# A neighbourhood-attention block whose TensorE program for attention becomes a loop

## What is computed

```python
x = x + attention(layernorm(x))         # 12 heads of 16; each query sees its 7 x 7 neighbourhood and 16 registers
t = x.reshape(-1, 192)
n = layernorm(t)
gate = softmax(n @ gate_w.T)            # 16 experts, the best two per token
y = sum over those two of gate * w2[e] @ (silu(w1[e] @ n) * (w3[e] @ n))
z = sw2 @ (silu(sw1 @ n) * (sw3 @ n))   # shared expert, 1024 wide
out = t + y + z
```

## Time and profile before

| | |
|---|---|
| median of three runs | 1367.69 us (1355.18 to 1371.36) |
| profiled execution | 1353.01 us, its span 1351.2 us |
| TensorE busy, share of the span | 1183.0 us, 88% |
| VectorE, ScalarE, POOL busy | 481.2, 364.4, 571.4 us |
| mean granted TensorE clock | 0.887 |
| transfers | 160.81 MB, mean 119 GB/s |

### The profile page before, as it was taken

The page is one execution under the profiler, slowest core; times in us unless marked ns, Lnnn a source line. Parts: engine busy times, 40 slices in busy tenths (PEclk is TensorE's granted clock), DMA queues, the critical chain, the costliest instruction groups (busy, mean ns, idle before and its releaser), DMA issues. The chain is left out here.

```text
span 1351.2 us, 41755 instructions
## 1 busy us (share of the span) xinstructions
PE 1183.0 (88%) x17206; PEld 962.0 (71%) x17206; DVE 481.2 (36%) x1066; ACT 364.4 (27%) x1271; POOL 571.4 (42%) x688
## 2 busy tenths in 40 slices
PE   5874886986888788788899999999999999999991
PEld 3432675775776676675576767769999999999991
DVE  3432543553554555456622222222222222222220
ACT  2322533443443434341111111111222222222220
POOL 4633543353544535310066660002555555554542
PEclk9987776676877878678999999999999999999996
DMA  5866325225262343310001121235888888888864
GB/s 129 175 163 152 70 69 95 57 68 90 67 106 59 86 87 98 90 41 16 9 17 36 36 83 43 64 122 141 223 221 229 220 221 228 215 220 217 218 162 120
DMA packets 126392, 160.81 MB, mean 119 GB/s; under 512 B 31936, under 2 KB 97248, under 8 KB 126016
## 3 DMA queue, kind: packets, MB, share of 16 engines
q1 hardware_dynamic: 104576, 137.18, 36.9%
q0 software_dynamic: 20336, 20.81, 9.9%
q10 hardware_dynamic: 1296, 0.17, 0.1%
HBM read 129.89 MB, written 31.83 MB: 120 GB/s over the span
## 5 line engine op out<-in xcount | busy, mean ns | idle before, releaser
L679 POOL DMA_INDIRECT acc_dram<-ys,lists x87 | 137.7, 1583 | 283.1 <-DVE ys L1068 180.2
L1357 PE MATMUL ps<-xa,w13r 128*128 128x128 f32 x1392 | 169.7, 275 | 0.3 <-ACT xa L790 0.3
L744 ACT ACTIVATE probs<-ps,nmax 128x156 f32<-128x156 f32 x432 | 162.7, 403 | 8.7 <-DVE nmax L885 8.4
L1357 PEld LDWEIGHTS ps<-xa,w13r 128*128 128x128 f32 x1392 | 162.3, 192 | 0.5 <-issue 0.5
L1061 DVE TENSOR_TENSOR m_h<-m_sg,ps 128x512 f32<-128x512 f32 x87 | 59.8, 688 | 288.8 <-ACT m_sg L796 288.8
L1279 PE MATMUL ps<-xT_all,sw13a_sb 64*128 64x384 f32 x768 | 145.9, 491 | 4.8 <-DVE s_h L1034 4.5
L1162 PE MATMUL ps<-kd,qr 28*32 28x156 f32 x3456 | 102.2, 360 | 46.2 <-issue 40.4
L564 POOL TENSOR_TENSOR kd<-kr,maskp 128x420 f32<-128x420 f32 x144 | 140.3, 1008 | 0.0
L1373 PE MATMUL ps<-w_sb,m_h 128*128 x696 | 136.4, 339 | 0.0
L885 DVE TENSOR_REDUCE nmax<-ps 128x6 f32<-128x936 f32 x72 | 81.5, 1132 | 120.1 <-PE ps L1162 118.9
L1373 PEld LDWEIGHTS ps<-w_sb,m_h 128*128 128x128 f32 x696 | 110.7, 189 | 10.7 <-issue 0.3
(11 more groups left out here) (151 smaller groups left out, 1553.7 us busy)
## 6 DMA issues: line engine op xcount, KB each, us to landing
w13r<-in_w13a SPq DMA_DIRECT2D x87, 512.0 KB
w13r<-in_w13b SPq DMA_DIRECT2D x87, 256.0 KB
vm<-v_dram SPq DMA_DIRECT2D x144, 94.5 KB
w_sb<-in_w SPq DMA_DIRECT2D x8, 768.0 KB, 4.8
vr<-v_dram SPq DMA_DIRECT2D x144, 42.0 KB
kr<-k_dram SPq DMA_DIRECT2D x24, 198.0 KB, 6.5
xn_dram<-xn SPq DMA_DIRECT2D x36, 128.0 KB, 2.8
a_x<-in_x SPq DMA_DIRECT2D x12, 288.0 KB, 3.5
```

Of the source, the lines that this page charges most:

```text
L679: nc.gpsimd.indirect_dma_start(acc_dram, bass.IndirectOffsetOnAxis(ap=lists[:, j, 0:1], axis=0), ys[:, j % V8, :], None, compute_op=ALU.ad ...
L744: ins = nc.scalar.activation(probs[:, n % 2, h, :], ps[:, 2 * half + b, NKEY * g:NKEY * (g + 1)], ACT.Exp, bias=nmax[:, half, b, g:g + 1], ...
L1357: mm(ps[:, g + k, 128 * f:128 * (f + 1)], w13r[:, j % RING, k, 128 * f:128 * (f + 1)], xa[:, j % 2, 0:128], start=f == 0, stop=False, skip ...
```

## The change

TensorE's turns 4 to 33 become a loop (`pe.Fori`) over pairs of turns, with four turns ahead of it and five behind written out. Buffer numbers must repeat after two tiles for that, so `kd`, `vm`, `vr` and `xn2` become two deep. Waits in the loop compare with registers that count tiles. Queries no longer come by the band with pattern rows in place. ScalarE writes them tile by tile into `a_q`, SP, ScalarE and POOL store them to a `q_dram` that has all 128 rows of each tile, the pattern rows are written there once, and one transfer a tile brings 128 full rows to `qt`. The gate's product is formed with the gate as the weight that is held and tokens as what streams, so that no address of a held weight depends on a register; it lands as 16 x 128 in `gT`, and 36 transposes at the end give `logits`. In SP's list x of band n+3 stands ahead of the stores of band n, values are loaded at band 6 for two tiles, and the shared expert's weights have a place of their own and are loaded before attention instead of at turn 30. The diff, cut to its core:

```diff
-        kr = [place("kr0", [128, 3, KBAND], f32, at)]
-        qr = [place("qr0", [128, 3, NC * 128], f32, at)]
-        early = at[0]
-        kr.append(place("kr1", [128, 3, KBAND], f32, at))
-        qr.append(place("qr1", [128, 3, NC * 128], f32, at))
-        kd = place("kd", [128, 3, 4, 3, NKEY], f32, at)
-        vm = place("vm", [128, 3, 4, D], f32, at)
-        vr = place("vr", [128, 3, 4, D], f32, at)
+        sw13a_sb = place("sw13a_sb", [128, 2, SINTER], f32, at)
+        sw13b_sb = place("sw13b_sb", [128, SINTER], f32, at)
+        sw2_sb = place("sw2_sb", [128, 8, D], f32, at)
+        after_sw = at[0]
+        kr = [place(f"kr{u}", [128, 3, KBAND], f32, at) for u in range(2)]
+        qt = place("qt", [128, 2, 3, 128], f32, at)
+        kd = place("kd", [128, 2, 4, 3, NKEY], f32, at)
+        vm = place("vm", [128, 2, 4, D], f32, at)
+        vr = place("vr", [128, 2, 4, D], f32, at)
...
+        def store_q(eng, j, a, g):
+
+            at0 = 64 * (a % 2) + HD * g
+            eng.dma_start(q_dram[NC * j:NC * (j + 1), 32 * g:32 * g + HD, a, :].rearrange("c d y -> d c y"),
+                          a_q[at0:at0 + HD, j % 2, a // 2, :, :]).then_inc((a_sqp if a == 2 else a_sq)[j % 2], 16)
+
+        def queries_stored(eng, j):
+            eng.wait_ge(a_sq[j % 2], A_SQ * (j // 2 + 1))
+            eng.wait_ge(a_sqp[j % 2], A_SQP * (j // 2 + 1))
...
-                u, j, half = n % 2, n // 2, 64 * (n % 2)
-                sp.wait_ge(a_ce[0], n + 1)
-                sp.dma_start(q_dram[0:128, j, :, half:half + 64],
-                             a_f[:, u, 0, :].rearrange("p (c y) -> p c y", c=NC)).then_inc(a_sto[u], 16)
+                u, at0 = n % 2, PADT + BAND * n
                 sp.wait_ge(a_ce[1], 2 * n + 2)
-                sp.dma_start(q_dram[128:192, j, :, half:half + 64],
-                             a_f[0:64, u, 1, :].rearrange("p (c y) -> p c y", c=NC)).then_inc(a_sto[u], 16)
-                at0 = PADT + BAND * n
-                sp.dma_start(k_dram[0:64, at0:at0 + BAND], a_f[64:128, u, 1, :]).then_inc(a_sto[u], 16)
+                sp.dma_start(k_dram[0:64, at0:at0 + BAND], a_k[64:128, u, 0, :]).then_inc(a_sto[u], 16)
                 sp.wait_ge(a_ce[2], n + 1)
-                sp.dma_start(k_dram[64:192, at0:at0 + BAND], a_f[:, u, 2, :]).then_inc(a_sto[u], 16)
+                sp.dma_start(k_dram[64:192, at0:at0 + BAND], a_k[:, u, 1, :]).then_inc(a_sto[u], 16)
                 sp.wait_ge(a_vev, 3 * n + 3)
                 sp.dma_start(v_dram[PADT + n * BAND:PADT + (n + 1) * BAND, :].rearrange("(s p) d -> p s d", p=128),
                              a_v[:, u, :, :]).then_inc(a_sto[u], 16)
@@ -386,31 +397,32 @@
                 if j == 0:
                     sp.wait_ge(s_pad, N_PAD)
                     sp.wait_ge(s_kz, 2)
-                    sp.wait_ge(s_qpat, 2)
                 if j >= 2:
                     sp.wait_ge(b_kd, NC * (j - 1))
-                    sp.wait_ge(b_S[0], NC * (j - 1))
-                    sp.wait_ge(b_S[1], NC * (j - 1))
                 for g in range(4):
                     sp.dma_start(kr[j % 2][32 * g:32 * g + HD, :, :],
                                  k_dram.rearrange("(a g d) t -> g d a t", a=3, d=HD)[
                                      g, :, :, QT * SIDE * j:QT * SIDE * j + KBAND]).then_inc(b_kld[j % 2], 16)
-                for g in range(4):
-                    sp.dma_start(qr[j % 2][32 * g:32 * g + HD, :, :],
-                                 q_dram.rearrange("(a g d) j c y -> g d a j (c y)", a=3, d=HD)[
-                                     g, :, :, j, :]).then_inc(b_qld[j % 2], 16)
+
+            def load_q(m):
+                if m % NC == 0:
+                    queries_stored(sp, m // NC)
+                if m >= 2:
+                    sp.wait_ge(b_S[0], m - 1)
+                    sp.wait_ge(b_S[1], m - 1)
+                sp.dma_start(qt[:, m % 2, :, :], q_dram[m]).then_inc(b_qld[m % 2], 16)
...
             for n in range(NB):
-                store(n)
                 if n + 3 < NB:
                     load_x(n + 3)
+                store(n)
+                if n % 2:
+                    for g in range(4):
+                        store_q(sp, n // 2, 0, g)
+                if n == 1:
+                    sp.wait_ge(s_qpat, 1)
+                    for g in range(4):
+                        sp.dma_start(q_dram[:, 32 * g + HD:32 * g + 32, :, :].rearrange("m p a y -> p m (a y)"),
+                                     pat_q[32 * g + HD:32 * g + 32, :].unsqueeze(1).broadcast_to([16, NT, 3 * 128])
+                                     ).then_inc(s_pq, 16)
...
                 if n == 4:
                     load_band(0)
                 if n == 5:
+                    sp.wait_ge(s_pq, 64)
+                    for m in range(2):
+                        load_q(m)
+                if n == 6:
+                    for m in range(2):
+                        load_v(m)
+                if n == 8:
                     for m in range(3):
                         load_patch(m)
-                if n == 7:
-                    for m in range(3):
-                        load_v(m)
             load_band(1)
...
+                if 2 <= n + 1 < NT:
+                    load_v(n + 1)
...
-                if m >= 3:
-                    pool.wait_ge(b_S[0], m - 2)
-                    pool.wait_ge(b_S[1], m - 2)
+                if m >= 2:
+                    pool.wait_ge(b_S[0], m - 1)
+                    pool.wait_ge(b_S[1], m - 1)
...
+                if n % 2:
+                    pool.wait_ge(a_ce[1], 2 * n + 2)
+                    for g in range(4):
+                        store_q(pool, n // 2, 2, g)
...
+                if u:
+                    act.wait_ge(a_ce[0], n + 1)
+                    for g in range(4):
+                        store_q(act, j, 1, g)
...
-                    v.tensor_copy(logits[:, n - 4, :], ps[:, 7, 448:448 + E]).then_inc(b_lg, 1)
+                    v.tensor_copy(gT[:, 128 * (n - 4):128 * (n - 3)], ps[0:E, 7, 0:128]).then_inc(b_lg, 1)
...
+            dve.wait_ge(b_lgT, 1)
+            v.tensor_copy(logits[:, 0:32, :], ps[:, 0, :].rearrange("p (n e) -> p n e", e=E))
+            v.tensor_copy(logits[:, 32:NT, :], ps[:, 1, 0:E * (NT - 32)].rearrange("p (n e) -> p n e", e=E)
+                          ).then_inc(b_logits, 1)
...
+            def scores(m, p, i, half):
+                if half == 0:
+                    pe.wait_ge(b_kd, m + 1)
+                    pe.wait_ge(b_qld[p], 16 * i + 16)
+                if type(m) is not int or m:
+                    pe.wait_ge(b_e[half], m)
+                pe.sem_inc(passed_pe, 1)
                 for g in range(3):
                     for a in range(4):
...
+            def gate(m):
+                pe.wait_ge(b_xTev, m + 1)
+                cols = ds(m * 128, 128)
+                mm(ps[0:E, 7, 0:128], gate_sb[:, 0, :], xT_all[:, 0, cols], start=True, stop=False)
+                mm(ps[0:E, 7, 0:128], gate_sb[:, 1, :], xT_all[:, 1, cols], start=False, stop=True).then_inc(b_G, 1)
...
+            def turn(n, k, i):
+
+                def is_tile(m):
+                    return type(m) is not int or 0 <= m < NT
+
+                t, u, w, nxt = n - 1, n - 2, n - 3, n + 1
+                i_t, i_nxt = (i - 1, i) if k == 0 else (i, i + 1)
+                if is_tile(t):
+                    probs_T(t, 1 - k, 0)
+                    probs_T(t, 1 - k, 1)
+                if is_tile(u):
+                    roots(u, k)
+                if is_tile(t):
+                    probs_T(t, 1 - k, 2)
+                    probs_T(t, 1 - k, 3)
+                if is_tile(nxt):
+                    scores(nxt, 1 - k, i_nxt, 0)
+                if is_tile(u):
                     project(u)
-                if 0 <= t < NT:
-                    values(t)
-                if 0 <= w < NT:
-                    token_T(w, u)
-                if n + 1 < NT:
-                    scores(n + 1, 1)
-                if 0 <= w < NT:
+                if is_tile(t):
+                    values(t, 1 - k, i_t)
+                if is_tile(w):
+                    token_T(w, 1 - k, u if is_tile(u) else None)
+                if is_tile(nxt):
+                    scores(nxt, 1 - k, i_nxt, 1)
+                if is_tile(w):
                     gate(w)
+
+            scores(0, 0, 0, 0)
+            scores(0, 0, 0, 1)
+            for n in range(4):
+                turn(n, n % 2, n // 2)
+            with pe.Fori(2, NT // 2 - 1) as i:
+                for k in range(2):
+                    turn(2 * i + k, k, i)
+            for n in range(NT - 2, NT + 3):
+                turn(n, n % 2, n // 2)
+
+            pe.wait_ge(b_lg, NT)
+            for m in range(NT):
+                ins = tr(ps[:, m // 32, E * (m % 32):E * (m % 32 + 1)], gT[:, 128 * m:128 * (m + 1)],
+                         ident_sb[0:E, 0:E])
+            ins.then_inc(b_lgT, 1)
```

221 lines of the change are left out of this document (100 added, 121 removed).

## The result

The changed kernel takes **1266.61 us** in the median (four runs, 1263.43 to 1270.45), the kernel before 1369.53 us (four runs, 1355.18 to 1386.82). The ratio is 0.928, with a 95% interval of 0.920 to 0.936. The forecast was 1245 us, between 1204 and 1325. The profiled execution has a span of 1266.5 us, against 1351.2. Some executions of a kernel are slower than its others by one per cent or more (the ninth experiment's profiled one is among them), and the ratios in this document leave those out, so that they differ a little from the quotient of the medians.

What follows compares the result with a forecast made beforehand. Bound: attention's 28 turns, where TensorE waits for 16 KB instruction blocks and its clock falls behind the stops. 1353.0 - 117 + 3 (loop entry) - 8 + 6 + 5 = 1242, forecast as 1245 us median, range 1204 to 1325.

Steps and rivals of the forecast that it cites:

- The loop: Attention's 28 turns: TensorE keeps the pass, a turn falls from 13.77 to 9.60 us, saving 117 us (66 to 138).
- nine more register and wait instructions: In each looped turn: extra instructions of the loop, taken at 0.76 us on top of 8.84 us.
- every pass misses: Rival, loop: each of 14 jumps back pays a block fetch, stops and clock stay; 1407 us, chance 0.13.
- The stops go and the clock stays: Rival, attention's turns: fetch stops vanish but the clock stays low, 12.0 us a turn; 1309 us, chance 0.19.
- Loads of x ahead of the stores: Projection: x asked for one store earlier, gain of 8 us, between 25 gained and 15 lost.
- the stop ahead of the eleventh band: Sign in projection: this TensorE stop should be gone if the forecast is right.
- the pattern transfers: Projection, band 1: four transfers, 3.54 MB, at least 13 us of all transfer engines, with x of band 5 queued behind.
- A stop near the fifth band: Sign in projection: a stop there may be new.
- pattern rows cost more: Rival, projection: x of band 5 late by 15 us, start of attention by 12; 1271 us, chance 0.06.
- Start of attention: Ahead of the first scores: POOL's last query stores, then keys, delay attention; +6 us, between 0 and 12.
- gate: End of attention: 36 transposes and two copies, uncovered; +5 us, at most 5.9 + 1.4 us.
- the weights ahead of tile 2's queries: Start of attention: 2 MB of shared weights stand ahead of these queries; 8 us, half of it hidden.

Runs made afterwards that it cites:

- the ninth experiment: Changed kernel with pattern rows written band by band from DRAM, shared weights in eleven pieces, token numbers earlier, normalising and POOL's last query stores later: 1240.20 us, ratio 0.902.
- the fifth experiment: Changed kernel with VectorE's two normalising instructions of a turn moved behind oT and the third copy of probabilities: 1252.81 us.
- Experiments 3 and 10: Changed kernel with a loop body of four turns: 1430.81 us; changed kernel with the scores' second half formed four times in looped turns: 1596.32 us.
- experiment 11: Changed kernel with one added wait ahead of project in each looped turn, for normalised tokens to land in DRAM, no fetch added: 1375.75 us.
- experiments 2 and 7: Changed kernel with pattern rows kept in SBUF and queries in four transfers: 1239.36 us; the same with x loaded behind the stores again: 1257.42 us.
- the fourth experiment: Changed kernel with VectorE's four steps on token numbers moved from behind the last band to band 8: 1267.55 us.

## Why the prediction was right, and where it was not

**The loop: right in mechanism, low in size.** TensorE keeps the pass, "issue" stops vanish, the queue moves 69 blocks, and the clock is 1.00. The 28 turns gave 129.8 us for a forecast of 117: 52.2 are stops (70.0 idle us became 17.8), 77.6 the clock, since the same matmuls went from 318.0 to 240.3 us. I had 9.60 us a turn, where 9.22 were measured: 8.84 and 0.76 for nine more register and wait instructions. Those cost nothing that shows, as the fifth experiment's 8.67 us with all of them tells. What does cost is 0.63 us of waiting for VectorE, the engine that I named as having the least room, but for a reason that I didn't see: its normalising is held by POOL's additions, so TensorE's turn hung on POOL's.

The Trainium skill, "SBUF — State Buffer", section "Who interferes with whom", says that `tensor_scalar` can enter a mode in which VectorE takes the port pair that it shares with GpSimd, and that whichever of the two starts second is blocked for the other's whole instruction. The rows agree in kind: 980 and 721 ns in the loop, 7.67 us at attention's start. The Trainium skill speaks of one instruction of the other engine; the 7.67 us spanned eight additions, and no run here shows why none of the gaps between them let VectorE in.

**The jump back: the rival's rule was real, its condition was not met.** I gave *every pass misses* 0.13 because no row told what is kept. Experiments 3 and 10 show it at 12 and at 9 blocks; at 7 it doesn't occur. The Trainium skill, "Runtime: NRT & Kernel Launch", section "Instruction fetch mechanics", gives TensorE's instruction memory 2048 instructions in one sentence, and in another, on taken branches of any engine, a window of two pages. The 1306 instructions that stayed speak against two pages; the 1882 that were fetched anew on nine blocks show that the number of instructions alone doesn't decide. From the 128 KiB of the Trainium skill an estimate is eight blocks of the 16 KB in the earlier trace rows; the runs set what is kept between 7 and 9.

**The clock: right, and shown.** "The stops go and the clock stays" is refuted by the clock of 1.00, and experiment 11 shows the other side: stops of 55 us in all that fetch nothing cost another 50 us in slower matmuls.

**Loads of x ahead of the stores: the step that failed.** I took a gain of 8 us, from +25 to -15, and got a loss of 20.6 us in projection. The order of SP's list is worth 11 to 13 us by experiments 2 and 7, and the stop ahead of the eleventh band is gone, as I said; the value loads, now at band 6, leave one of 4.1 us ahead of the tenth. The mis-sized term is the pattern transfers: I priced 3.54 MB at the last stage's 206 GB/s, "at least 13 us", and used that lower bound as the upper end too. The transfers moved with everything else 113 GB/s at a share of 0.90, and the stop was 38.2 us. The row that I took has large pieces into 128 partitions; these were pieces of 1536 bytes out of 16. A stop near the fifth band was among the signs that I listed, and the rival *pattern rows cost more* had the place; its 1271 us lie nearer the result than my 1245, but with 23 us lost in projection where 28.6 us were missing, and without the turns' extra gain.

**Start of attention and gate: near in size, one for the wrong reason.** +7.5 us for +6 at the start, but the query stores ahead of POOL's keys were not what TensorE waited for; it was VectorE's held instruction. My other term there, the weights ahead of tile 2's queries, cost nothing in the changed kernel, where TensorE came no earlier than the queries; the fourth experiment shows it at 6.05 us of stop. (2 MB at 206 GB/s are 9.7 us, not the 8 that I wrote.) The end cost 11.5 us for 5. Between the last `project` and the shared expert are 13.5 us against 6.6, and the 36 transposes are most of that, with the copies behind them:

```profile
534.26 4.02 PE L1324 MATMUL ps<-ident_sb,gT 16*128 16x16 f32 x36 [0.37 <-DVE gT L937]
539.19 1.65 PE L1338 MATMUL ps<-xT_all,sw13a_sb 64*128 64x384 f32 x4 [0.91 <-DVE logits L1082]
```

That is 6.9 us for the gate, within its bounds. The other 4.6 us of the end are in the written-out turns behind the loop, which are fetched and stop as before; why they took 29.8 us where they had taken 25.2, no run shows.

By the table the span lies 26.3 us above the forecast's sum: 28.6 in projection, 1.5 at the start, 2.3 in the first turns, 6.5 at the end and 0.2 behind it, less 12.8 gained in the turns. So the forecast was near in part by luck: a gain in the turns that I had too small made up for nearly half of the loss in projection that I had not seen.

## What to carry to other kernels

Where TensorE stops in the middle of runs of small matmuls with nothing late, count the blocks that its program moves, and make the repeating part a loop that lies on few of them: here seven stayed, nine did not, and a body too long cost more than none. Count such a stop twice, once as time and once as clock. And price a new transfer by a row with the same pieces, the same number of partitions and the same direction; bytes over the best rate in sight is only a lower bound.
